# State space stage of a four-layer kernel: sums over the states of three token tiles moved from VectorE and GpSimd to accumulating transfers

## The reference, cut to what matters

```python
    uc = _silu(conv3(u) + conv_b)                 # u, z: halves of x @ W_in.T
    x_dbl = jnp.einsum('blh,eh->ble', uc, W_xproj)     # dtp (64), Bm (16), Cm (16)
    dt = jax.nn.softplus(jnp.einsum('blr,hr->blh', dtp, W_dt) + b_dt)
    A = -jnp.exp(A_log)
    def step(h, inp):
        u_t, dt_t, B_t, C_t = inp
        dA = jnp.exp(dt_t[:, None, :] * A[None, :, None])
        h = dA * h + B_t[:, :, None] * u_t[:, None, :]
        y_t = jnp.einsum('bn,bnh->bh', C_t, h)
        return (h, y_t)
    y = jnp.moveaxis(ys, 0, 1) + D * uc
    y = y * _silu(z)
    out = jnp.einsum('blh,dh->bld', y, W_out)
    return x + out
```

## Time and profile before

| | |
|---|---|
| median of three runs | 3569.99 us (3563.14 to 3570.53) |
| profiled execution, span from the first to the last instruction | 3547.4 us (its total is not listed apart) |
| window of the state space scans | 37.3 to 905.4 us: 868.1 us, 128 steps |
| busy over the span | TensorE 94%, VectorE 68%, GpSimd 49%, ScalarE 44% |
| busy in the scan stage | VectorE 850.1 us, TensorE 756.6, GpSimd 748.7, ScalarE 653.6 |
| granted TensorE clock, mean over the span | 0.985 of full speed |

### The profile page before, as it was taken

One profiled execution on the slowest core, in us unless ns is written; L12 is line 12 of the kernel. 1 busy time (PEld: TensorE's weight loads), 2 busy tenths in 40 slices (PEclk: granted clock), 3 DMA queues, 4 the chain that ended last, 5 costly groups with the idle time before them and its releaser, 6 DMA issues. The chain is left out here.

```text
span 3547.4 us, 59663 instructions
## 1 busy us (share of the span) xinstructions
PE 3336.7 (94%) x21120; PEld 2437.0 (69%) x21120; DVE 2409.3 (68%) x5247; ACT 1564.9 (44%) x3124; POOL 1736.2 (49%) x2205
## 2 busy tenths in 40 slices
PE   7888988888589999999999989999999999999999
PEld 5666666666468888888876656666655566666565
DVE  8999999999655555555554447777733377777332
ACT  6887778876242222222221125555511255555111
POOL 6988889888450000000012237777611277777221
PEclk9999999999789999999999999999999999999999
DMA  4011101111441000010012211112121111121121
GB/s 143 1 62 62 62 1 62 62 56 46 146 125 37 13 10 13 10 37 12 12 36 74 81 60 37 37 37 60 30 74 54 60 32 38 37 72 31 61 65 35
DMA packets 166972, 176.13 MB, mean 50 GB/s; under 512 B 22756, under 2 KB 150264, under 8 KB 166296
## 3 DMA queue, kind: packets, MB, share of 16 engines
q1 hardware_dynamic: 163272, 162.94, 14.2%
q0 software_dynamic: 3408, 9.38, 0.7%
HBM read 94.19 MB, written 78.09 MB: 49 GB/s over the span
## 5 line engine op out<-in xcount | busy, mean ns | idle before, releaser
L3087 ACT ACTIVATE win_probs<-win_sc,win_nbias,tile_rn 128x256 f32<-128x256 f32 x512 | 282.3, 561 | 311.7 <-DVE win_nbias L3171 311.7
L438 POOL TENSOR_TENSOR ssm_acc<-ssm_acc,ssm_weighted 128x512 f32<-128x512 f32 x255 | 339.0, 1339 | 101.4 <-ACT ssm_weighted L587 100.7
L424 POOL TENSOR_SCALAR ssm_ub<-ssm_uT,ssm_bcT 128x512 f32<-128x512 f32 x512 | 359.1, 725 | 21.8 <-PE ssm_pu L1151 18.0
L1151 PEld LDWEIGHTS ssm_pu<-ident,ssm_ub 128*128 128x128 f32 x2048 | 237.6, 142 | 184.9 <-issue 87.0
L3273 PE MATMUL win_pa<-win_w_wqkv,tile_hT 128*128 128x512 f32 x744 | 360.9, 622 | 0.0
L1151 PE MATMUL ssm_pu<-ident,ssm_ub 128*128 128x128 f32 x2048 | 308.4, 279 | 51.0 <-DVE ssm_state L821 33.8
L1998 POOL TENSOR_TENSOR lin_rstd<-lin_mv,lin_eps 128x1 f32<-128x1 f32 x30 | 5.7, 190 | 667.5 <-DVE lin_mv L173 667.5
L1167 PE MATMUL ssm_pt<-ident,ssm_state 128*128 128x128 f32 x2040 | 278.1, 278 | 48.4 <-DVE ssm_acc L831 30.3
L821 DVE TENSOR_TENSOR_SCAN ssm_state<-ssm_da,ssm_carry,ssm_pu 128x512 f32<-128x512 f32 x256 | 312.5, 1261 | 2.3 <-ACT ssm_da L575 2.3
L2689 PE MATMUL glu_up<-block_hT,glu_w_w 128*128 128x512 f32 x704 | 305.7, 592 | 3.4 <-DVEq L88 3.4
L821 DVE TENSOR_TENSOR_SCAN ssm_state<-ssm_da,ssm_pu 128x512 f32<-128x512 f32 x256 | 296.8, 1200 | 4.9 <-PE ssm_pu L1151 2.7
(11 more groups left out here) (422 smaller groups left out, 7399.4 us busy)
## 6 DMA issues: line engine op xcount, KB each, us to landing
sorted_rows<-block_zeros SPq DMA_DIRECT2D x8, 4290.0 KB, 15.8
block_wide<-x SPq DMA_DIRECT2D x18, 512.0 KB, 6.6
tile_raw<-in_tables SPq DMA_DIRECT2D x64, 128.0 KB, 2.2
a<-tile_y SPq DMA_DIRECT2D x64, 128.0 KB, 1.7
block_wide<-a SPq DMA_DIRECT2D x32, 256.0 KB, 3.3
block_x<-a SPq DMA_DIRECT2D x16, 512.0 KB, 5.3
block_x<-sorted_rows SPq DMA_DIRECT2D x39, 130.0 KB, 2.6
x<-block_more SPq DMA_DIRECT2D x16, 256.0 KB, 2.2
```

The lines of the kernel that those rows point to most:

```text
L424: nc.gpsimd.tensor_scalar(ub[:, i % 2, t, :], uT[:, k % 2, t, :], bcT[:, k % 2, t, n:n + 1], 1.0, ALU.mult, ALU.mult).then_inc(ub_ready.se ...
L438: nc.gpsimd.tensor_tensor(acc[:, k % 2, t, :], acc[:, k % 2, t, :], weighted[:, j, :], ALU.add)\
L1151: last = nc.tensor.transpose(pu[c][:, t * P:(t + 1) * P], ub[:, i % 2, t, c * P:(c + 1) * P], ident)
L3087: nc.scalar.activation(probs[:, head, :], sc[j][:, r, :], ACT.Exp, bias=nbias[:, g, j, r:r + 1], scale=rn[:, turn.side, 0, head:head + 1], ...
```

## The change

Of the four token tiles of a state, VectorE keeps the first (`add_first`, one instruction a step in place of two). ScalarE weighs tiles 1, 2 and 3 (three instructions in place of two) into a buffer of two steps. GpSimd adds none itself: it issues one transfer a tile, SBUF to SBUF with `accum_op=ALU.add`, that adds the weighted tile to `acc`; each waits for the weighing of its tile and for the landing of the same tile's transfer one step before. For the very last state VectorE does tiles 1 to 3 itself (`add_last`, three instructions in place of one). The PSUM banks are now freed by ScalarE three times in four. To make room, one of the two `weighted` buffers and `xd` lie in the memory that was `work`, `work` lies in `u` (so the column that the next block needs is kept aside earlier, `keep_left`), and the load of the experts' biases, whose place is that same memory, moves from the end of `following.load` to `load_experts`, which the next stage's program calls behind its weight loads.

```diff
+        work = u[:, :, 1:BLK + 1]
+        weighted = [memory.spare[:, 0:(TB - 1) * HID].rearrange("p (t h) -> p t h", h=HID), s.sb("weighted", [P, TB - 1, HID])]
+        xd = memory.spare[0:XR, (TB - 1) * HID:(TB - 1) * HID + BLK]
-        weighted = s.sb("weighted", [P, 2, HID])
...
-            def add_odd(i, j):
-                k, t = i // NS, 2 * j + 1
+            def add_weighted(i, t):
+                k, done = i // NS, added[t - 1]
                 if i % NS == 0:
-                    pool.wait_ge(begun.sem, begun.at(k))
-                pool.wait_ge(weighed.sem, weighed.at(i, j + 1))
-                pool.wait_ge(sums_odd.sem, sums_odd.at(i - 1, j + 1))
-                nc.gpsimd.tensor_tensor(acc[:, k % 2, t, :], acc[:, k % 2, t, :], weighted[:, j, :], ALU.add)\
-                  .then_inc(sums_odd.sem, 1)
+                    pool.wait_ge(begun.sem, begun.at(k, t + 1))
+                pool.wait_ge(weighed.sem, weighed.at(i, t))
+                if i:
+                    pool.wait_ge(done.sem, done.at(i - 1))
+                nc.gpsimd.dma_start(acc[:, k % 2, t, :], weighted[i % 2][:, t - 1, :], accum_op=ALU.add).then_inc(done.sem, 16)
...
-                if 0 <= i - 1 < N * NS:
-                    add_odd(i - 1, 0)
-                    if i < N * NS:
-                        add_odd(i - 1, 1)
+                if 0 <= i - 1 < N * NS - 1:
+                    for t in range(1, TB):
+                        add_weighted(i - 1, t)
...
-            def weigh(i, j):
-                k, t = i // NS, 2 * j + 1
-                act.wait_ge(state_turned.sem, state_turned.at(i, 2 * j + 2))
-                act.wait_ge(sums_odd.sem, sums_odd.at(i - 1, j + 1))
-                nc.scalar.activation(weighted[:, j, :], turned_bank(i, t)[:, :], ACT.Copy,
+            def weigh(i, t):
+                k = i // NS
+                act.wait_ge(state_turned.sem, state_turned.at(i, t + 1))
+                if i >= 2:
+                    act.wait_ge(added[t - 1].sem, added[t - 1].at(i - 2))
+                nc.scalar.activation(weighted[i % 2][:, t - 1, :], turned_bank(i, t)[:, :], ACT.Copy,
...
                 if 0 <= i - 1 < N * NS - 1:
-                    weigh(i - 1, 1)
+                    weigh(i - 1, 2)
+                    weigh(i - 1, 3)
...
+            def weigh_and_add(i, t):
+                k = i // NS
+                dve.wait_ge(state_turned.sem, state_turned.at(i, t + 1))
+                return nc.vector.scalar_tensor_tensor(acc[:, k % 2, t, :], turned_bank(i, t)[:, :],
+                                                      bcT[:, k % 2, t, NS + i % NS:NS + i % NS + 1], acc[:, k % 2, t, :],
+                                                      ALU.mult, ALU.add)
...
                 if behind:
-                    add_even(i - 1, 0)
+                    add_first(i - 1)
                 if scanning:
                     scan(i, 2)
                     scan(i, 3)
-                if behind:
-                    add_even(i - 1, 1)
...
-                j = t // 2 + 1
-                if i == N * NS - 1 and j == 2:
+                if t < 2:
+                    pe.wait_ge(weighed.sem, weighed.at(i - 1, t + 2))
+                elif i == N * NS - 1:
                     pass
-                elif t % 2:
-                    pe.wait_ge(weighed.sem, weighed.at(i, j - 1) if j == 2 else weighed.at(i - 1))
+                elif t == 2:
+                    pe.wait_ge(sums_first.sem, sums_first.at(i))
                 else:
-                    pe.wait_ge(sums_even.sem, sums_even.at(i, j - 1) if j == 2 else sums_even.at(i - 1))
+                    pe.wait_ge(weighed.sem, weighed.at(i, 1))
...
     def load_experts(self, sp):
+        sp.dma_start(self.m.expert_b[:, :], self.w["expert_b"].partition_broadcast(P)).then_inc(self.experts_in, 16)
```

62 lines of the change are left out of this document (31 added, 31 removed).

## The result

The changed kernel takes 3585.25 us (median of 5 runs, 3577.18 to 3587.49) against 3568.94 for the kernel before on the same chip: ratio 1.0042, 95% interval [1.0029, 1.0054]. It is slower by 0.4%, where 1% faster was forecast. The profiled execution has a span of 3584.0 us. All further runs were made on five chips. On four of them the kernel before takes 3550 to 3552 us and on the fifth 3567, so times are compared by their ratio to the kernel before on the same chip. On one of the four the changed kernel repeats the result: 3570.32, ratio 1.0046 [1.0029, 1.0063].

A forecast was written before the change was run, and what follows sets the result against it. VectorE bounds the kernel at 108.5 us a block; GpSimd, VectorE and ScalarE near full give 103. Gain 44 us less 9 (clears 4, last state 2, biases 3) is 35: span 3512, median 3535 us; range 3482 to 3650.

The forecast's parts named there:

- VectorE's need: Scan stage: fewer sums and less disturbed taps take VectorE's work from 107.2 to 96 us a block.
- ScalarE's loss: Scan stage: one more weighing a step adds 9.4 us a block, from 83.2 to about 93.
- The issue's price: GpSimd's time to issue one transfer: 1.0 us taken, bounds 0.96 and 1.27, 48 issues a block.
- GpSimd as the bound: Rival, scan stage: issues cost 1.27 us, blocks take 116 us, 3639 us in all; chance 0.24.
- with three near full I allow 1.4 above the largest: Scan stage: block length set at 103 us, 1.4 above GpSimd's need of 101.6, the largest of three engines.
- TensorE was put at nothing: Scan stage: TensorE gets no added instruction, has 12% of slack, and its banks being freed by ScalarE costs nothing.
- The clears: Scan stage: six clears of 15.8 us share the transfer engines and make transfers late: +4 us, ends 0 and +35.
- The price of an addition: Transfers inside SBUF: a tile takes 0.97 us of all engines as a copy, 1.9 if its old value is read.
- The tail: After the scans: last state's extra sums and landings +2 us, moved biases +3 us.
- The moved biases: Expert stage's loads: 1 MB of biases moves to a stretch where transfers are busy: +3 us, other end 0.
- The offset of 22.6 us: Whole kernel: the median of the runs lies 22.6 us above the profiled span, taken as unchanged.
- No change: Rival, scan stage: GpSimd issues `scale_u` too late each step, VectorE's saved time becomes idle: 3570 us; chance 0.08.

The follow-up runs named there:

- clears_first: Changed kernel with the six clears issued at the start with the other two, instead of one in each of blocks 1 to 6: ratio 1.0047.
- spread: Changed kernel with each clear cut into eleven pieces, one a state: 3547.42 us, ratio 0.9988.
- narrow_two: Changed kernel with each accumulating transfer cut to one column and the third one not issued: ratio 0.9906.
- narrow_all: Changed kernel with transfers of one column, the third one not issued, and tile 3's weighing cut to one column: 3502.37 us, ratio 0.9867.
- spread_order: spread with ScalarE's copy of hidden rows moved ahead of two weighings and GpSimd's fourth begin_sum one step later: 3555.24 us, ratio 0.9968.
- narrow_dma: Changed kernel with each accumulating transfer adding one column instead of 512; issues, waits and weighings stay: ratio 0.9957.
- pair: Kernel before with only GpSimd's two sums made accumulating transfers; VectorE keeps two sums, ScalarE two weighings: 3541.30 us, ratio 0.9970.

## Why the prediction was wrong

**VectorE's need: right.** 775.5 / 8 = 97 us a block, where 96 was forecast. Its busy share of the stage was to fall from 98% to about 93 and fell to 87. The taps' median fell from 858 ns to 752, most of the 0.13 us given.

**ScalarE's loss: right.** 72.1 us in the stage, 9.0 a block, where 9.4 was forecast; its need is 91.

**The issue's price: too high, in the changed kernel's disfavour.** 0.88 us by the ends, below the lower bound of 0.96 from the indirect rows. GpSimd needs 53.6 + 48 x 0.88 = 96 us a block, not 101.6. So the rival with the largest share, GpSimd as the bound from 1.09 upwards, did not happen, although the time lies on its side. The Trainium skill (DMA: Bandwidth & Descriptors, Anatomy of one DMA) calls this part "small, variable"; here it is 42 us of a block of 115 on one engine, and not small.

**The step that failed** is "with three near full I allow 1.4 above the largest". The largest need was 97 us. Without the clears' cost the block is 109.7 (clears_first and spread), 13 above. By the two repeated spans the kernel lost 28 us where 35 of gain were forecast, 63 apart: 6 x (109.7 - 103) = 40 of them are this step, 32 - 4 = 28 the clears, and the first and last block give some 5 back. The allowance was taken from a kernel with one full engine, whose neighbours always had time to be early. The windows of the earlier trace rows were used for ScalarE and VectorE alone, and gave 105.3; GpSimd's two `begin_sum`, its three issues and TensorE's place behind both queues were never laid beside each other in one step. TensorE was put at nothing, because it "waited little for either engine". It then waited 40 us for `scale_u` where it was 12, and 31 for the weighings where it was 15, and VectorE 71 us for the tiles that TensorE turned (54.8 + 16.3), where it was 9.5. narrow_two, narrow_all and spread_order show that it is what stands in these queues, and its order, that costs: 1.6 us a block for the third issue in step 2, 1.1 more there for the third weighing, and 2.0 in step 2 by moving alone, of which 0.9 is left over the block. That accounts for a part of the 13. Of the rest, some 7 stay open (narrow_all).

**The clears: right in mechanism, too small.** +4 was taken, with +35 as the other end; measured are 4.5 x 6 = 27 in step 11 alone and 32 by whole blocks. A little over half a us of lateness was allowed per clear; an addition beside one is 4.2 us late in the median, and the "landings under 6 us" that were to hide become 8.5. A clear takes some 15 us to land by itself, which was a reason to take more. The price of an addition, 0.97 to 1.9 us of all engines, was well put: (0.164 x 3572.5 - 25) / 381 = 1.47, and 0.68 for a plain copy; the 25 us are the queue's other work, 0.7% of the span before.

**The tail: right in sum, by luck.** +4 measured for +5, but not from the terms named. The moved biases, +3 of it, can hardly be seen: narrow_dma and pair, which have them, come to 139.7 and 140.2 us from the last scan to the next layer, against 138.9. On the quicker chips the kernels with three whole additions in the last block come to 143 to 146, so the wait for the last landings is nearer +4 than the +2 taken.

**The offset of 22.6 us** between the median and the profiled span was taken as unchanged; in the changed kernel it is 1.3. It did no harm, since it was added to a difference of spans, but it was no property of the kernel (see the distance of 159.5 us above).

**The range held, the sign did not.** The range was wide enough for rivals that did not happen, so that it held says little. "No change" was described nearly rightly, GpSimd issuing `scale_u` too late so that VectorE's gain becomes waiting, and given 0.08. It is what happened, though mostly in two steps of a block and not in each, with the clears on top.
